# Writing out the loops of a metaformer kernel, with fewer small VectorE steps per strip

## The reference, cut to what matters

```python
x = x + window_attention(ln(x))     # 8x8 shifted windows, 8 heads, bias table, softmax
t = t + routed_ffn(ln(t))           # scores = ln(t) @ wr + br; the best half of each image
                                    # gets gelu(h @ w1 + b1) @ w2 + b2, times its score
x = x + conv3x3(quantized ln_c(x))
t = t + graph_experts(ln_t(t))      # graph attention over 524288 random edges gives scores,
                                    # the two best of 4 experts per token are mixed
```

## Time and profile before

| | us |
|---|---|
| median of 3 runs | 10940.03 (10927.17 to 10954.37) |
| the profiled execution, its own time | 10950.05 |
| its span, first to last instruction | 10948.2 |
| VectorE busy / GpSimd busy / TensorE busy / ScalarE busy | 5565.9 / 6207.5 / 4602.7 / 3954.9 |
| mean TensorE clock granted | 0.728 of full speed |

### The profile page before, as it was taken

One profiled execution on the slowest core, in us unless ns is written; L12 is line 12 of the kernel. 1 busy time (PEld: TensorE's weight loads), 2 busy tenths in 40 slices (PEclk: granted clock), 3 DMA queues, 4 the chain that ended last, 5 costly groups with the idle time before them and its releaser, 6 DMA issues. The chain is left out here.

```text
span 10948.2 us, 130025 instructions
## 1 busy us (share of the span) xinstructions
PE 4602.7 (42%) x31813; PEld 2736.9 (25%) x31813; DVE 5565.9 (51%) x14498; ACT 3954.9 (36%) x9657; POOL 6207.5 (57%) x6259
## 2 busy tenths in 40 slices
PE   0011777777775998874232222322323323223000
PEld 0011555555553544551111111111101101101000
DVE  9987999999996776551211211212212112112477
ACT  0011877777782554332121211212212212112255
POOL 0000545444451222666777777777777777777675
PEclk9755999999897999876666666666666666666555
DMA  0000111111112222553222222222222222222366
GB/s 21 0 0 36 38 34 37 37 38 37 37 34 85 62 61 75 145 136 60 45 49 44 45 48 44 47 45 46 47 44 47 48 41 49 47 41 49 137 239 242
DMA packets 1325947, 662.48 MB, mean 61 GB/s; under 512 B 1058256, under 2 KB 1239101, under 8 KB 1320765
## 3 DMA queue, kind: packets, MB, share of 16 engines
q1 hardware_dynamic: 1142396, 576.49, 19.3%
q0 software_dynamic: 183104, 80.22, 6.2%
HBM read 344.86 MB, written 313.71 MB: 60 GB/s over the span
## 5 line engine op out<-in xcount | busy, mean ns | idle before, releaser
L1838 POOL DMA_INDIRECT gr_rec<-rec,gr_idx x4096 | 3960.0, 967 | 1248.8 <-issue 1247.9
L1859 PE MATMUL gr_p_h<-gr_tT,gr_w 128*128 128x512 f32 x1568 | 847.2, 695 | 3678.2 <-ACT gr_hT L1893 3646.2
L1978 DVE TENSOR_SCALAR gr_pen<-gr_same 128x64 f32<-128x64 f32 x64 | 13.5, 211 | 3168.1 <-DMA gr_rec<-rec,gr_idx 3168.1
L546 POOL TENSOR_TENSOR at_sq<-at_qk 128x256 f32<-128x256 f32 x392 | 294.2, 750 | 1972.9 <-ACT at_qk L595 1972.3
L1859 PEld LDWEIGHTS gr_p_h<-gr_tT,gr_w 128*128 128x128 f32 x1568 | 347.8, 227 | 4159.1 <-ACT gr_hT L1893 3731.3
L1906 ACT ACTIVATE gr_ee<-gr_dd 128x512 f32<-128x512 f32 x64 | 40.3, 629 | 3595.9 <-DVE gr_dd L1997 3595.9
L1864 PE MATMUL gr_p_y<-gr_hT,gr_w 128*128 128x512 f32 x1568 | 688.9, 592 | 0.0
L1958 DVE STREAM_TRANSPOSE gr_z<-gr_yb 128x2048 f32<-128x2048 f32 x98 | 226.5, 2311 | 893.9 <-ACT gr_yb L1898 863.2
L1893 ACT ACTIVATE gr_hT<-gr_p_h,gr_b 128x512 f32<-128x512 f32 x784 | 517.7, 688 | 189.4 <-PE gr_p_h L1859 186.1
L2146 POOL DMA_INDIRECT cb_a<-scan,cb_idx x392 | 503.0, 1283 | 133.6 <-issue 121.0
L1342 POOL DMA_INDIRECT adst<-co_rec,co_idx x448 | 422.9, 944 | 218.9 <-issue 146.6
(11 more groups left out here) (364 smaller groups left out, 13064.6 us busy)
## 6 DMA issues: line engine op xcount, KB each, us to landing
y<-gr_z SPq DMA_DIRECT2D x392, 256.0 KB, 5.2
cb_y<-y SPq DMA_DIRECT2D x28, 3584.0 KB, 13.1
gr_rec<-rec,gr_idx POOLq DMA_INDIRECT x4096, 2.4
scan<-gr_out SPq DMA_DIRECT2D x64, 768.0 KB
at_xs<-in_x_win SPq DMA_DIRECT2D x56, 448.0 KB, 3.8
x<-at_x SPq DMA_DIRECT2D x56, 448.0 KB, 4.4
ff_x<-x SPq DMA_DIRECT2D x56, 448.0 KB, 3.3
x<-ff_x SPq DMA_DIRECT2D x784, 32.0 KB
```

Of the source, the lines that this page charges most:

```text
L546: nc.gpsimd.tensor_tensor(sq[r][:, :], qk[r][:, :], qk[r][:, :], ALU.mult).then_inc(S["sq"], 1)
L1838: nc.gpsimd.indirect_dma_start(out=rec[s][:, j, :], out_offset=None, in_=rec_dram, in_offset=bass.IndirectOffsetOnAxis(ap=idx[s][:, j:j + ...
L1859: nc.tensor.matmul(p_h[m % 4][:, :], w1[:, P * m:P * (m + 1)], tT[b.k][:, :], start=True, stop=True).then_inc(S["hp"], 1)
```

## The change

All loops of `pairs_of` and `trips` become Python loops, so that the instruction streams are written out from end to end and every wait value and address is a constant. The two small loops in `Bias.sync` stay. `bn_aggr` writes mean and variance of a strip straight into `stats_sb`, ScalarE turns the variance into the reciprocal deviation in place, and the two copies of `score` go. The search compares with the node numbers where they lie, without the copy to `q`; the last arithmetic step of each level writes its result in int32 (or to `rp`), without the cast or copy behind it. The next level reads the index as int32. No gather, matmul or large transfer is added, dropped or moved.

```diff
@@ -356,9 +356,7 @@
         lnv = [sb(f"lnv{i}", [P, PPS]) for i in range(2)]
         rstd = [sb(f"rstd{i}", [P, PPS]) for i in range(2)]
         wst = [sb(f"wst{i}", [P, PPS, 6]) for i in range(2)]
-        wmv = [sb(f"wmv{i}", [P, PPS, 2]) for i in range(2)]
         wln = [sb(f"wln{i}", [P, PPS]) for i in range(2)]
-        wrs = [sb(f"wrs{i}", [P, PPS]) for i in range(2)]
         wdot = [sb(f"wdot{i}", [P, PPS]) for i in range(2)]
         wtmp = [sb(f"wtmp{i}", [P, 2, PPS]) for i in range(2)]
         junk = [sb(f"junk{i}", [P, C]) for i in range(2)]
@@ -405,7 +403,7 @@
 
             for u in range(-4, HALF):
                 emit(Step(eng, u, u, 0, 0, True, False))
-            with eng.Fori(1, STRIPS // 2 - 1) as i:
+            for i in range(1, STRIPS // 2 - 1):
                 for u in range(HALF):
                     emit(Step(eng, u, i * HALF + u, i * 2, i, False, False))
             for u in range(HALF + 3):
@@ -568,9 +566,10 @@
 
                 def wrstd(s, strip):
                     act.wait_ge(S["wstat"], strip + 1)
-                    nc.scalar.activation(wln[s][:, :], wmv[s][:, :, 1], ACT.Ln, bias=eps[:, 1:2]).then_inc(S["wrstd"], 1)
+                    var = stats_sb[:, bass.ds(strip * PPS, PPS), 1]
+                    nc.scalar.activation(wln[s][:, :], var, ACT.Ln, bias=eps[:, 1:2]).then_inc(S["wrstd"], 1)
                     act.wait_ge(S["wrstd"], 2 * strip + 1)
-                    nc.scalar.activation(wrs[s][:, :], wln[s][:, :], ACT.Exp, scale=-0.5).then_inc(S["wrstd"], 1)
+                    nc.scalar.activation(var, wln[s][:, :], ACT.Exp, scale=-0.5).then_inc(S["wrstd"], 1)
 
                 def emit(p):
                     if p.u == 0 or p.u == -4:
@@ -680,14 +679,13 @@
                 def score(s, strip):
 
                     v.wait_ge(S["wrstd"], 2 * (strip + 1))
-                    nc.vector.scalar_tensor_tensor(wtmp[s][:, 0, :], wmv[s][:, :, 0], nswr[:, 1:2], wdot[s][:, :],
+                    cols = bass.ds(strip * PPS, PPS)
+                    nc.vector.scalar_tensor_tensor(wtmp[s][:, 0, :], stats_sb[:, cols, 0], nswr[:, 1:2], wdot[s][:, :],
                                                    ALU.mult, ALU.add).then_inc(S["score"], 1)
                     v.wait_ge(S["score"], 3 * strip + 1)
-                    nc.vector.tensor_tensor(wtmp[s][:, 1, :], wtmp[s][:, 0, :], wrs[s][:, :], ALU.mult).then_inc(S["score"], 1)
+                    nc.vector.tensor_tensor(wtmp[s][:, 1, :], wtmp[s][:, 0, :], stats_sb[:, cols, 1], ALU.mult).then_inc(S["score"], 1)
                     v.wait_ge(S["score"], 3 * strip + 2)
-                    nc.vector.tensor_copy(stats_sb[:, bass.ds(strip * PPS, PPS), 0], wmv[s][:, :, 0])
-                    nc.vector.tensor_copy(stats_sb[:, bass.ds(strip * PPS, PPS), 1], wrs[s][:, :])
-                    nc.vector.tensor_scalar(score_sb[:, bass.ds(strip * PPS, PPS)], wtmp[s][:, 1, :], consts[:, 4:5], None,
+                    nc.vector.tensor_scalar(score_sb[:, cols], wtmp[s][:, 1, :], consts[:, 4:5], None,
                                             ALU.add).then_inc(S["score"], 1)
 
                 def emit(p):
@@ -761,7 +759,7 @@
                             p.wait("dot", -3)
                             v.sem_inc(S["passed"], 1)
                             for j in range(PPS):
-                                ins = nc.vector.bn_aggr(wmv[s][:, j, :], wst[s][:, j, :])
+                                ins = nc.vector.bn_aggr(stats_sb[:, bass.ds(strip * PPS + j, 1), :].rearrange("p o k -> p (o k)"), wst[s][:, j, :])
                             ins.then_inc(S["wstat"], 1)
                             if p.last and p.u == HALF + 2:
                                 score(s, strip)
@@ -933,7 +931,7 @@
 
     for t in range(-ahead, peel * span):
         emit(Trip(eng, sems, count, span, t // span, t % span))
-    with eng.Fori(peel, count // span - 1) as i:
+    for i in range(peel, count // span - 1):
         for u in range(span):
             emit(Trip(eng, sems, count, span, i, u))
     for t in range(count - span, count + behind):
@@ -1485,7 +1483,7 @@
         self.ids = sb("ids", [P, NPP])
         self.heads = sb("heads", [P, P])
         self.rp = sb("rp", [P, NPP])
-        self.q, self.c0, self.c1, self.c2, self.r0, self.r1 = (two(n, [P, PPS]) for n in ("q", "c0", "c1", "c2", "r0", "r1"))
+        self.c0, self.c1, self.c2 = (two(n, [P, PPS]) for n in ("c0", "c1", "c2"))
         self.i0, self.i1 = (two(n, [P, PPS], I32) for n in ("i0", "i1"))
         self.got0, self.got1 = (two(n, [P, PPS, BLK]) for n in ("got0", "got1"))
         self.junk = sb("junk", [P, PPS, P])
@@ -1533,8 +1531,8 @@
 
     def gather_firsts(self, pool, at, cols):
         s = at[1] % 2
-        self.wait(pool, "lv0", at, 5)
-        self.wait(pool, "lv1", at, 5, back=2)
+        self.wait(pool, "lv0", at, 3)
+        self.wait(pool, "lv1", at, 4, back=2)
         pool.sem_inc(self.S["passed"], 1)
         for j in cols:
             self.nc.gpsimd.indirect_dma_start(out=self.got0[s][:, j, :], out_offset=None, in_=self.first_dram,
@@ -1542,16 +1540,20 @@
 
     def gather_blocks(self, pool, at, cols):
         s = at[1] % 2
-        self.wait(pool, "lv1", at, 5)
-        self.wait(pool, "lv2", at, 4, back=2)
+        self.wait(pool, "lv1", at, 4)
+        self.wait(pool, "lv2", at, 3, back=2)
         pool.sem_inc(self.S["passed"], 1)
         for j in cols:
             self.nc.gpsimd.indirect_dma_start(out=self.got1[s][:, j, :], out_offset=None, in_=self.blocks,
                                               in_offset=bass.IndirectOffsetOnAxis(ap=self.i1[s][:, j:j + 1], axis=0)).then_inc(self.S[f"block{s}"], 16)
 
-    def below(self, q, table):
+    def strip_of(self, table, at):
+        return table[:, bass.ds((at[0] * 2 + at[1]) * PPS, PPS)]
+
+    def below(self, at, table):
         n = table.shape[-1]
-        return self.nc.vector.tensor_tensor(self.junk[:, :, 0:n], table, q[:, :].rearrange("p (j o) -> p j o", o=1).to_broadcast([P, PPS, n]), ALU.is_lt)
+        q = self.strip_of(self.ids, at).rearrange("p (j o) -> p j o", o=1).to_broadcast([P, PPS, n])
+        return self.nc.vector.tensor_tensor(self.junk[:, :, 0:n], table, q, ALU.is_lt)
 
     def count(self, out, n):
         return self.nc.vector.tensor_reduce(out[:, :], self.junk[:, :, 0:n], AX_X, ALU.add)
@@ -1559,40 +1561,32 @@
     def partition_of(self, v, at):
         s, S, vec = at[1] % 2, self.S, self.nc.vector
         self.wait_gathers(v, "first", at, back=2)
-        vec.tensor_copy(self.q[s][:, :], self.ids[:, bass.ds((at[0] * 2 + at[1]) * PPS, PPS)]).then_inc(S["lv0"], 1)
-        self.wait(v, "lv0", at, 5, 1)
-        self.below(self.q[s], self.heads[:, :].rearrange("p (o n) -> p o n", o=1).to_broadcast([P, PPS, P])).then_inc(S["lv0"], 1)
-        self.wait(v, "lv0", at, 5, 2)
+        self.below(at, self.heads[:, :].rearrange("p (o n) -> p o n", o=1).to_broadcast([P, PPS, P])).then_inc(S["lv0"], 1)
+        self.wait(v, "lv0", at, 3, 1)
         self.count(self.c0[s], P).then_inc(S["lv0"], 1)
-        self.wait(v, "lv0", at, 5, 3)
-        vec.tensor_scalar(self.r0[s][:, :], self.c0[s][:, :], 1.0, 0.0, ALU.subtract, ALU.max).then_inc(S["lv0"], 1)
-        self.wait(v, "lv0", at, 5, 4)
-        vec.tensor_copy(self.i0[s][:, :], self.r0[s][:, :]).then_inc(S["lv0"], 1)
+        self.wait(v, "lv0", at, 3, 2)
+        vec.tensor_scalar(self.i0[s][:, :], self.c0[s][:, :], 1.0, 0.0, ALU.subtract, ALU.max).then_inc(S["lv0"], 1)
 
     def block_of(self, v, at):
         s, S, vec = at[1] % 2, self.S, self.nc.vector
         self.wait_gathers(v, "first", at)
         self.wait_gathers(v, "block", at, back=2)
-        self.below(self.q[s], self.got0[s][:, :, :]).then_inc(S["lv1"], 1)
-        self.wait(v, "lv1", at, 5, 1)
+        self.below(at, self.got0[s][:, :, :]).then_inc(S["lv1"], 1)
+        self.wait(v, "lv1", at, 4, 1)
         self.count(self.c1[s], BLK).then_inc(S["lv1"], 1)
-        self.wait(v, "lv1", at, 5, 2)
+        self.wait(v, "lv1", at, 4, 2)
         vec.tensor_scalar(self.c1[s][:, :], self.c1[s][:, :], 1.0, 0.0, ALU.subtract, ALU.max).then_inc(S["lv1"], 1)
-        self.wait(v, "lv1", at, 5, 3)
-        vec.scalar_tensor_tensor(self.r1[s][:, :], self.r0[s][:, :], float(EP // BLK), self.c1[s][:, :], ALU.mult, ALU.add).then_inc(S["lv1"], 1)
-        self.wait(v, "lv1", at, 5, 4)
-        vec.tensor_copy(self.i1[s][:, :], self.r1[s][:, :]).then_inc(S["lv1"], 1)
+        self.wait(v, "lv1", at, 4, 3)
+        vec.scalar_tensor_tensor(self.i1[s][:, :], self.i0[s][:, :], float(EP // BLK), self.c1[s][:, :], ALU.mult, ALU.add).then_inc(S["lv1"], 1)
 
     def edge_of(self, v, at):
         s, S, vec = at[1] % 2, self.S, self.nc.vector
         self.wait_gathers(v, "block", at)
-        self.below(self.q[s], self.got1[s][:, :, :]).then_inc(S["lv2"], 1)
-        self.wait(v, "lv2", at, 4, 1)
+        self.below(at, self.got1[s][:, :, :]).then_inc(S["lv2"], 1)
```

(7 more changed lines are left out.)

## The result

The changed kernel takes 10784.87 us (median of 4 runs, 10780.35 to 10791.85) against 10942.22 us for the kernel before on the same chip: a ratio of 0.9857 with a 95% interval of 0.984 to 0.9874, 157 us less. The forecast was 202 us less, so the direction and the range held, and the kernel gave 45 us less than the sum, 78% of it.

The account below looks back on a forecast made before the run. VectorE was taken to bound attention, GpSimd's gathers graph, TensorE the routed network. Terms of 82, 19, 25, 65, 8 and 3 sum to 202 us off the profiled 10950: 10748, or 10738 as the median; range 10680 to 10840.

Parts of the forecast that it names:

- Step 1: Attention: VectorE's stalls by issue at the loop's jump back go, 82 us less.
- Rival A: Attention: the pause belongs to the instruction stream, not the jump, and stays elsewhere; 101 us less in all, 10839; 13%.
- Step 2: Attention: VectorE's wait for ScalarE in the first pair after a jump goes, 19 us less, at least 10.
- Step 3: Attention: VectorE's waiting for register steps in the loop goes, 25 us less, from 0 to 54.
- Step 4: Attention: six small copies and casts less per strip on VectorE, 65 us less, from 37 to 88.
- Step 5: Attention: ScalarE rises from 79% to 87% busy, a thinner cover; part of the register and small-step gains may be lost.
- Steps 6 to 8: Other stages: routed network 0, convolution's waits for stores 8, graph 0, combine's register steps 3 us less.
- Rival B: Convolution: a shorter chain of stores lets GpSimd run through, up to 49 us more gain, about 10660 to 10700; 10%.
- Rival C: Short loops written out turn into instruction streams, making the kernel slower; 6%.

Follow-up runs that it names:

- Experiments 7 and 9: 7: attention's loop written out on TensorE 10923.98, VectorE 10915.55, both 10858.12 us; 9: its body doubled, 10913.38 us; all against the kernel before.
- attn_loop: The kernel before with attention's loop alone written out on all engines, all small steps kept: 10841.59 us, ratio 0.9905.
- stats_only: The kernel before with all loops written out and statistics aggregated straight into the table, search as before: 10826.59 us, ratio 0.9896.
- loops_only: The kernel before with all loops written out and all small steps kept: 10832.49 us, ratio 0.9899.
- experiment 5: The changed kernel without ScalarE's table load at the top of every 14 pairs of attention, one at the start kept: 10764.46 us.

## Why the prediction came out as it did

*What bounds the kernel* held: VectorE in attention, gathers in graph. The gathers kept their 944 ns.

*Step 1, the stall at the jump, 82 us,* held. The last pair of an iteration, the one in front of the jump, went from 6.85 to 3.57 us in the median (differences of the starts of at_lg), 3.28 us for each of the 25 jumps (the last of the 26 iterations has none behind it). Experiments 7 and 9 show that it belongs to the jump, and that TensorE and VectorE each pay their own. In the loop of the kernel before, from 1150 to 3220 us, the waits by "issue" of over 1 us are 25 of VectorE's, all at L704, 25 of TensorE's, all at L479, none of ScalarE's, and 7 of GpSimd's, 1.4 to 1.9 us each at L1540. Rival A is out.

*Step 2, the refill, 19 us,* failed, and it is nearly half of attention's shortfall of 41 us. I read 19.3 us of waiting for ScalarE in the first pair and called it TensorE and ScalarE coming back late. Only 5.3 us of it lie in the loop, less than the 10 that I gave as the least. The lateness itself was there, and worth about what I took: with TensorE alone written out the first pair is 0.71 us shorter, 18 us in all. But in the changed kernel it was 0 us of gain: the pair takes 6.2 us before and 6.1 after. The table load at the same place held VectorE up once the jump no longer did. It was in the trace, 29 loads of 1283 ns, one per iteration, and the code names it at the top of `emit`. I never asked what ScalarE did in that pair. Without it the pair takes 5.4 us, and attention is 25 us shorter.

*Step 3, register steps, 25 us,* held: steps 1 and 3 were to bring 107 us and the loop alone brought 103. From the kernel before to attn_loop the twelve pairs between the first and the last of an iteration take 0.94 us less together (means), 24 us over 26 iterations; the rest is step 1, less 4 us by which the first pair grew. The stretching beside GpSimd is in the trace: in the kernel before, from 1240 to 3200 us, at_xh (L717) takes 332 to 368 ns where at_sq (L546) does not run beside it, and up to 1035 where it does; at_qkn (L726) takes 409 to 462 ns, and up to 857.

*Step 4, small steps, 65 us,* was mis-sized: 46 us from attn_loop to the changed kernel. Of the price of 0.21 us each, the search's four steps kept 41 us of 47 when written out (from stats_only to the changed kernel, in attention). The two copies brought 8 us of 18 by the rows of experiment 8. They stood between two dependent steps, where the third (L690) waits for the second in any case; part of their time was cover for that wait. In the looped kernel they and their register steps did make that distance 0.36 us longer (0.56 against 0.20), near the forecast's 0.32, but 0.21 us of it went with the loop and belongs to step 3. Together that is 49 us, between the 46 from attn_loop and the 52 from loops_only; profiles of like kernels differ by as much. In the changed kernel at_oT waited 10 us by "issue" (1.7 before), which belongs to step 2: it went with the table loads (experiment 5).

*Step 5, ScalarE as the thinner cover,* was the right worry without its price: ScalarE was busy 62.7 us in an iteration of 74 us, as forecast, and did not run out of time on the whole. It was late in one pair of 14.

*Steps 6 to 8* came to -11 us by forecast and to -8 by the four stages, by other parts: combine gave 12.5 and the convolution nothing. TensorE's jump in the routed network was hidden: in the kernel before, matmuls go on through the 207 to 228 ns of the branch at each of its 25 jumps (L936), and TensorE has no idle time there nor in the 0.5 us behind it. *Rival B* is out: VectorE's wait for the stores of the convolution fell from 114.3 us in 34 times to 94.9 in 23, and the stage did not get shorter. *Rival C*, that the written-out short loops pay for their fetches, is out as well. From 3500 to 4200 us q8 moves 1 block in the kernel before and 21 in the changed one. Over the routed network it is now 25, over the convolution 21:

```profile
q8 instruction: 25, 0.41, 0.2%
```

(DMA queues of the changed kernel, 3300 to 4100 us; the 21 are of 4200 to 4780 us). The fetches cost little: TensorE's longest wait by "issue" in front of L1051 is 0.8 us, the same as in the kernel before, and the routed network is 4 us longer. No run shows blocks of these stages that come as late as the code behind a jump of attention; at 3748 ns each, the 25 would have been 94 us. Whether the fetches make these 4 us, or the convolution's 7, was not tried. In attention TensorE's loop costs fetches of its own: from 1240 to 3150 us q8 moves 216 blocks in the kernel before, 219 with VectorE alone written out and 165 with TensorE alone written out, about seven per 14 pairs.

## What to carry to other kernels

A loop with a long body can cost an engine a pause at its jump, once per jump; here it was 3.2 us on VectorE and 3.7 on TensorE at the same time, none on ScalarE, with about nine blocks of 16 KB fetched per iteration. With the short bodies of the other stages TensorE's branch took 0.2 us. Write out (or lengthen the body of) all the engines that pause together: one alone brought 24 or 30 us of 95. Before you count such a gain, read what every other engine does in the pair behind the pause: a table load or a wait that it covered is late next, as at_rs was here (5.3 us of waits in the loop before, 28.4 written out). A small step between two dependent ones can be worth less than its length, since it fills a wait: the two copies of 0.17 and 0.16 us brought 0.15 per strip, and moving the dependent steps apart earned about as much (0.18).

## What the runs showed of the hardware that I had not expected

TensorE's branch at the long body's end takes 3748 ns in its own row, while VectorE's branch has a row of 68 ns and its 3.2 us appear as idle time by "issue" behind it: the pause has to be looked for in both places. And a pause that two engines make at the same time is worth far more than the sum of single cures suggests: 24 and 30 us alone, 95 together, and of the 30 only 3 were the pause.
